# Another order of the steps between two groups of heads, in the attention of layer 1

## The reference

```python
xn = _layernorm(x)
q = xn @ wq.T; k = xn @ wk.T; v = xn @ wv.T      # 32, 8 and 8 heads of 128
q = q * cos + _rotate_half(q) * sin              # k alike
scores = (q @ k^T) / sqrt(128) * scale + causal  # 1024 x 1024 for each head
probs = softmax(scores)
x = x + (probs @ v) @ wo.T + _L1_ffn_ref(xn, ...)
```

## Time and profile before

| | us |
|---|---|
| median of 3 runs | 1768.2 |
| lowest and highest | 1765.95 and 1768.75 |
| the profiled execution, its own time | 1769.56 |
| its span in the profile | 1767.8 |

### The profile page before, as it was taken

The page is one execution under the profiler, slowest core; times in us unless marked ns, Lnnn a source line. Parts: engine busy times, 40 slices in busy tenths (PEclk is TensorE's granted clock), DMA queues, the critical chain, the costliest instruction groups (busy, mean ns, idle before and its releaser), DMA issues. The chain is left out here.

```text
span 1767.8 us, 32007 instructions
## 1 busy us (share of the span) xinstructions
PE 1646.9 (93%) x10959; PEld 1273.1 (72%) x10959; DVE 1112.4 (63%) x1898; ACT 709.1 (40%) x1483; POOL 819.2 (46%) x808
## 2 busy tenths in 40 slices
PE   5788999997889999999999999999999999979999
PEld 4444444456778878878878878878878878867887
DVE  6877788324866766676676676676576576544333
ACT  4435556751155145145245235335325325432221
POOL 4087999400643553553453453364354354134331
PEclk9989999999999999999999999999999999989999
DMA  6440000001110000000000010001001001012101
GB/s 128 55 67 3 2 2 2 3 14 35 41 31 13 19 25 19 19 25 19 19 25 19 13 31 19 13 20 30 8 18 36 1 18 55 1 48 66 42 14 48
DMA packets 36054, 47.05 MB, mean 27 GB/s; under 512 B 11757, under 2 KB 18125, under 8 KB 35901
## 3 DMA queue, kind: packets, MB, share of 16 engines
q1 hardware_dynamic: 35922, 45.11, 10.5%
HBM read 37.56 MB, written 2.10 MB: 22 GB/s over the span
## 5 line engine op out<-in xcount | busy, mean ns | idle before, releaser
L1566 DVE TENSOR_TENSOR ptnl<-ps,ptnh 128x512 fp32r<-128x512 f32 (+1 forms) x320 | 204.0, 638 | 136.2 <-ACT ptnh L1484 130.2
L1484 ACT ACTIVATE ptnh<-ps 128x512 fp32r<-128x512 f32 (+1 forms) x320 | 177.8, 556 | 268.6 <-PE ps L1410 265.9
L71 PE MATMUL ps<-xth,wh 128*128 128x512 f32 (+1 forms) x560 | 225.6, 403 | 5.7 <-POOL wl L2027 4.1
L73 PE MATMUL ps<-xth,wl 128*128 128x512 f32 (+1 forms) x560 | 222.8, 398 | 0.0
L72 PE MATMUL ps<-xtl,wh 128*128 128x512 f32 (+1 forms) x560 | 222.7, 398 | 0.0
L1554 DVE TENSOR_REDUCE negm<-ps 128x1 f32<-128x768 f32 (+3 forms) x224 | 183.5, 819 | 34.6 <-PE ps L1388 32.0
L71 PE MATMUL ps<-ptnh,vh 128*128 128x256 f32 x576 | 183.7, 319 | 10.7 <-DVE ptnl L1566 10.2
L1656 POOL TENSOR_SCALAR pshort<-pshort,rinv 128x128 f32<-128x128 f32 (+3 forms) x64 | 34.4, 537 | 277.0 <-DVE rinv L1591 277.0
L73 PE MATMUL ps<-ptnh,vl 128*128 128x256 f32 x576 | 161.3, 280 | 0.0
L72 PE MATMUL ps<-ptnl,vh 128*128 128x256 f32 x576 | 160.7, 279 | 0.0
L718 ACT ACTIVATE pt<-ps 128x512 f32<-128x512 f32 x226 | 131.4, 596 | 70.8 <-PE ps L509 45.2
(11 more groups left out here) (225 smaller groups left out, 3870.0 us busy)
## 6 DMA issues: line engine op xcount, KB each, us to landing
raw<-in_w SPq DMA_DIRECT2D x48, 256.0 KB, 2.6
raw<-in_wo SPq DMA_DIRECT2D x32, 256.0 KB, 2.6
qstack<-qpart SPq DMA_DIRECT2D x40, 128.0 KB, 5.3
raw<-in_gate_main SPq DMA_DIRECT2D x10, 256.0 KB, 2.7
raw<-in_up_main SPq DMA_DIRECT2D x10, 256.0 KB, 2.8
raw<-in_down_main SPq DMA_DIRECT2D x10, 256.0 KB, 2.6
resid<-in_x SPq DMA_DIRECT2D x4, 512.0 KB, 5.4
out<-resid SPq DMA_DIRECT2D x8, 256.0 KB, 2.0
```

The lines of the kernel that those rows point to most:

```text
L71: pe.matmul(out, lh, rh, start=first, stop=False)
L73: return pe.matmul(out, ll, rh, start=False, stop=last)
L1484: nc.scalar.activation(ptnh[:, i % PT_RING, 0:w], ps[:, b, 0:w], ACT.Copy).then_inc(high_ready, 1)
L1566: nc.vector.tensor_tensor(ptnl[:, i % PT_RING, 0:w], ps[:, b, 0:w], ptnh[:, i % PT_RING, 0:w].bitcast(F32), ALU.subtract).then_inc(low_rea ...
```

## The change

Three things move, and one wait is loosened. The first score fill of the next group stands directly behind the last projection; it now waits for the rotation of projection 9 alone (`8 + 2 * n`), which frees banks 0 and 1. The two output products stand between the score fills, and the two vturns behind them. The sixth score fill, `qk5`, stands in the next list behind its first two turns. The loop's body now ends with `proj9 proj10 proj11 qk0 out6 qk1 qk2 out7 qk3 vturn0 qk4 vturn1`, the next list begins with `wo0 wo1 wo2 wo3 turn0 turn1 qk5 av0 turn2 av1 turn3 qk6 av2 turn4 av3 turn5 qk7`, and `first_steps` ends with `proj11 qk0 vturn0 qk1 vturn1 qk2 qk3 qk4`. Nothing is added or taken out.

```diff
--- before.py
+++ after.py
@@ -1110,6 +1110,9 @@
 NTOK = len(PAIRS) // 2
 
 
+CARRIED = 2 * AHEAD - 1
+
+
 def group_steps(more):
 
     turns = [("turn", u) for u in range(NUNIT)]
@@ -1119,6 +1122,7 @@
         if u + 2 < NUNIT:
             main[j].append(turns[u + 2])
     out = [("wo", i) for i in range(G1)] + turns[:2]
+    out.append(("qk", 2 * AHEAD - 1))
     for j in range(NPAIR):
         side = []
         if j + AHEAD < NPAIR:
@@ -1136,11 +1140,17 @@
                 if f % NB == NB - 1 and f // NB + W_RING < NCHUNK:
                     side.append(("w", f // NB + W_RING))
         out += interleave(main[j], side)
-    out.append(("out", NTOK - 2))
-    if more:
-        out += [("vturn", 0), ("vturn", 1)] + [("qknext", n) for n in range(2 * AHEAD)]
-    out.append(("out", NTOK - 1))
-    return out
+    outs = [("out", NTOK - 2), ("out", NTOK - 1)]
+    return out + (change(outs) if more else outs)
+
+
+def change(outs=()):
+
+    nxt = [("qknext", n) for n in range(CARRIED)]
+    turns = [("vturn", 0), ("vturn", 1)]
+    if outs:
+        return [nxt[0], outs[0], *nxt[1:3], outs[1], nxt[3], turns[0], nxt[4], turns[1], *nxt[5:]]
+    return [nxt[0], turns[0], nxt[1], turns[1], *nxt[2:]]
 
 
 def first_steps():
@@ -1150,7 +1160,7 @@
         out.append(("proj", f))
         if f % NB == NB - 1 and f // NB + W_RING < NCHUNK:
             out.append(("w", f // NB + W_RING))
-    return out + [("vturn", 0), ("vturn", 1)] + [("qknext", n) for n in range(2 * AHEAD)]
+    return out + change()
 
 
 BANK_KINDS = ("turn", "vturn", "out")
@@ -1375,7 +1385,7 @@
                 if n >= 2:
                     pe.wait_ge(exp_ready, g * NHEADS + (n - 1))
                 else:
-                    pe.wait_ge(rope_read, g * 10 + 10)
+                    pe.wait_ge(rope_read, g * 10 + (8 + 2 * n))
                     pe.wait_ge(vt_ready, g * 2 + 2)
                 pe.wait_ge(kq_ready, g * 10 + (2 * h + 4))
                 q = (qth[:, h, t * P:(t + 1) * P], qtl[:, h, t * P:(t + 1) * P])
```

## The result

The changed kernel takes 1788.95 us (median of 4 runs, 1787.02 to 1793.05), the kernel before 1767.08 beside it (1764.71 to 1768.75). The ratio is 1.0131, with a 95% interval from 1.0117 to 1.0145: slower by 1.3%, where 1786.8 us was forecast. The quotient here is 1.0124.)

The account below looks back on a forecast made before the run. PE, busy for 93% of the span, was taken as the bound: 1769.56 + 9.0 (boundaries) + 9.6 (clock) = 1788.2 us as profiled, 1786.8 against the median of 1768.2. Forecast 1781 to 1793; range without the ends 1776 to 1797.

Parts of the forecast that it names:

- The place: Boundary, ahead of the sixth turn: POOL scales pair 2 behind four `wo` splits, a wait of about 3.5 us.
- The walk: PE, DVE and POOL timed through the boundary: sixth turn at 25.5 us, seven boundaries 178.5 against 171.1, +7.4.
- the clearing: Last boundary: the clearing of 0.52 us now lies ahead of the splits, so on the path, +0.5.
- The first boundary: Boundary behind `first_steps`: sixth turn at 24.6 us against 23.52, +1.1.
- The clock: Behind the sixth turn: one fall of TensorE's clock at each of eight boundaries, 1.2 us each, +9.6.
- the sign: Stretch behind the boundaries: 113 to 114 us instead of 112.29, with a granted clock below 1.00.
- The wait without the clock's price: Rival: POOL's hole is there, but the slow stretches fall into it; 1768.2 + 9.0 = 1777.2 us, chance 0.22.
- Two long falls behind each wait: Rival: the clock stays low for two stretches behind each wait; 1768.2 + 9.0 + 22.7 = 1799.9 us, chance 0.13.
- POOL is not late: Rival: pair 2 is scaled when its exponential is done, sixth turn at about 22 us; 1751 us, chance 0.05.
- the third chunk comes in time: Rival, no change: splits 1.16 us less at eight boundaries, 9.3, cancels the 9.0; clock costs nothing; chance 0.05.

Follow-up runs that it names:

- filled wait: The changed kernel with 13 extra matmuls of 512 columns on PE ahead of the wait for the sixth turn: 1781.92 us, ratio 1.0068.
- half and half: The changed kernel with `wo0` and `wo1` ahead, `wo2` and `wo3` behind the third turn (also called two splits behind): 1756.09 us, ratio 0.9936.
- the loop written out: The half and half kernel with seven copies of the layer 1 loop body in place of the loop: 1745.69 us, ratio 0.9873; the kernel before, likewise: 1766.85 us.
- one split behind: The changed kernel with only the last `wo` split moved behind the third turn: 1765.57 us, ratio 0.9992.
- the new order alone: The changed kernel with the sixth score fill back at the end of the list of before, behind `vturn1`: 1759.44 us, ratio 0.9964.

## Why the prediction was right

**The place.** The step on which all hung was that POOL scales pair 2 behind the four splits, and that this, not PE, sets the sixth turn. The trace after shows it directly, and three edits test it: moving one split takes 1.98 us from the boundary, moving two or four takes 3.0 to 3.2, and then the wait left in front of the sixth turn is 0.4 to 0.5 us, for a scaling that starts as soon as its reciprocals are there; moving the fill back takes the wait away altogether. Moving only the fill brings it without the rest of the change.

**The walk.** Forecast and measured, in us behind the last projection's last matmul, for the second boundary: maximum of `qk0` 3.56 and 3.54, addition of `out7` 9.58 and 9.64, reciprocals of pair 0 10.19 and 10.25, maximum of `qk4` 12.0 and 11.98, reciprocals of pair 1 13.15 and 13.12, first split 14.2 and 14.20, pair 2 at 23.28 and 23.10, sixth turn 25.5 and 25.37. One step of it was wrong and cost nothing: the first turn was to start at 12.8, and starts at 14.3, behind the jump; PE has slack there, since POOL comes later still. The wait in front of the sixth turn, forecast at about 3.5, is 3.37 (3.0 to 3.4 in the six groups of the loop, 4.1 ahead of them and 5.75 at the last). The seven boundaries sum to 178.8 us, with 178.5 and 0.5 for the clearing forecast; against 171.1 that is +7.7. The last is 26.95, 1 us above what was forecast for it: the fourth chunk also came late there.

POOL at the last boundary, the fourth split:

```profile
1477.42 0.62 POOL L1612 TENSOR_SCALAR woh<-raw 128x512 fp32r<-128x512 f32 x1 [1.18 <-DMA raw<-in_wo]
```

The first boundary came out at 24.35 in place of 24.6, +0.8. That is +8.5 for the +9.0 that the prediction had.

**The clock.** This term was too small. The seven stretches behind the sixth turns sum to 799.9 us, against 7 x 112.29 = 786.0, and the last, with the rest of the kernel, is 306.17 against 305.71 (a window on the trace of before, 1462.09 to 1767.80). That makes +14.4 where the term had 9.6. I had taken one fall of the clock behind each wait with a price of 1.2 us; it stays low for longer, and the price is 1.05 at the first, 1.8 to 2.3 at the six others and 0.5 at the last. The stretches, at 114.05 to 114.61 in these six, so lie above the 113 to 114 that I had named as the sign. The filled wait shows that this is the clock's and nothing else's.

**What hid the error.** The part ahead of the first boundary ended at 478.63 us in place of 481.46, 2.8 earlier, with the same program. In the eleven other traces it ends between 476.7 and 484.2, so it is the spread of single executions. 8.5 + 14.4 - 2.8 = 20.1 us, the whole difference of the spans. The mechanism was right in both its parts, but that the sum came so near (1788.2 for the profiled execution, which took 1789.7) is in part luck: 4.8 us too little for the clock met 2.8 of spread and 0.5 too much for the boundaries.

**The rivals.** The wait without the clock's price (1777.2) fell with the windows at 0.52. Two long falls behind each wait (1799.9) were too many: the 14.4 us lie between its 22.7 and my 9.6, nearer to mine. That POOL is not late is wrong, and that the third chunk comes in time too: it was awaited for 1.02 us.

## What to carry to other kernels

When one list is the program order of all engines, moving a step moves what it carries on every engine, its late parts too. Look on each engine for what the step is now behind and when its result is due: here a fill that PE could well do later brought a scaling of 2.2 us behind 9 us of work that nobody was waiting for yet. Where such a step has to move, the block is better cut in pieces and set around the work that is due; neither all of it ahead nor all of it behind did (1788.95 and 1768.53 us), and half and half was faster than both (1756.09). To leave the fill in its place did about as well (1759.44). And a loop's body should end in work that an engine can still do while its sequencer jumps: with the loop written out the kernel took 1745.69 us. Last, count a long wait on PE twice, once for its length and once for the clock behind it.

## What the runs showed of the hardware

The clock's fall depended on the length of the wait and on what lay around it. Waits of 3.0 us and more lowered it in every group of the changed kernel, to 0.50 to 0.66 of full speed over the 5 us that followed; waits of 2.25 and 2.73 us did so too, and one in six did at 1.1 to 1.5 us. With two splits behind, the waits ahead of a group's first turn lowered it where they were 1.9 to 2.3 us long (four groups) and not at 1.65 and 1.80; with one split behind none of 1.8 to 2.1 us did. The price of a wait can so be more than half of its length again: 1.8 to 2.3 us behind 3.0 to 3.4. Thirteen matmuls whose results nobody uses, put into the wait, bought back 14 us behind the turns, and the kernel was 7 us faster for having them. A fall inside a boundary cost 1.4 us before. With the splits cut in two the boundaries with a fall are 1.8 to 2.0 us longer (24.12 to 24.36 for 22.3), of which 0.2 to 0.5 is a longer wait ahead of the first turn and 1.5 to 1.6 comes behind it.

The jump back of a loop was the other surprise: PE idle for 1.6 to 2.3 us in the new order, 0.6 without the jump, nothing to be seen of it in the old order. It cost little by itself (0.6 us of a boundary with two splits behind, nothing to be seen in the new order alone), and more by the falls of the clock that came with it.
